# Gated linear attention and ternary FFN on one core: o is transposed and measured before it is centred and gated, and two transposes move up in TensorE's order

## The reference, cut to what matters

```python
q, k, v = x @ Wq, x @ Wk, x @ Wv                      # 16 heads of 8
gate = exp(log_sigmoid(x @ Wgk1 @ Wgk2 + bgk2) / 16)
state = state * gate[..., None] + v[..., None] * k[..., None, :]   # over the 512 tokens
o = einsum('bhvk,bhk->bhv', state, q)
o = (o - mean(o)) / sqrt(var(o) + 1e-5) * gamma + beta             # over the 128 channels
r = (o * silu(x @ Wg)) @ Wout
x2 = layernorm(x + r)
f1 = silu(x2 @ w1 * s1) * (x2 @ w2 * s2)              # 512 wide
f2 = gelu(f1 @ h1 * s3); f3 = gelu(f2 @ h2 * s4)
out = layernorm(x2 + f3 @ w3 * s5)
```

## Time and profile before

| | |
|---|---|
| median of 3 runs | 179.19 us (178.98 to 179.69) |
| profiled execution | 179.29 us, of which 177.5 are the span of the profile |
| TensorE (PE) busy | 160.9 us, 91% of the span |
| VectorE (DVE) busy | 141.6 us, 80% |
| ScalarE (ACT) busy | 110.2 us, 62% |
| GpSimd (POOL) busy | 109.4 us, 62% |
| granted TensorE clock | full speed in all of the span |

### The profile page before, as it was taken

The page is one execution under the profiler, slowest core; times in us unless marked ns, Lnnn a source line. Parts: engine busy times, 40 slices in busy tenths (PEclk is TensorE's granted clock), DMA queues, the critical chain, the costliest instruction groups (busy, mean ns, idle before and its releaser), DMA issues.

```text
span 177.5 us, 2647 instructions
## 1 busy us (share of the span) xinstructions
PE 160.9 (91%) x778; PEld 119.3 (67%) x778; DVE 141.6 (80%) x306; ACT 110.2 (62%) x179; POOL 109.4 (62%) x97
## 2 busy tenths in 40 slices
PE   0899999999879999999899999989999999999980
PEld 0766657868657666877666778567666875887870
DVE  0689989968898997698999987999998895854062
ACT  4454889992147635478683508667935388995722
POOL 8705998969609689970577989609684420803132
PEclk9999999999999999999999999999999999999999
DMA  3999920244200000000000000000020000041112
GB/s 109 284 380 416 398 91 0 59 122 118 59 4 0 0 2 0 4 2 0 0 0 0 0 0 0 0 0 0 0 63 0 0 2 0 0 104 32 34 31 63
DMA packets 7455, 10.55 MB, mean 59 GB/s; under 512 B 753, under 2 KB 5394, under 8 KB 6930
## 3 DMA queue, kind: packets, MB, share of 16 engines
q1 hardware_dynamic: 6866, 7.50, 13.9%
q0 software_dynamic: 576, 2.88, 4.2%
HBM read 8.55 MB, written 1.84 MB: 58 GB/s over the span
## 4 chain that ended last, share of the span: by engine, by line
DVE 21%; PE 19%; issue 14%; ACT 6%; POOL 3%; DVEq 1%; POOLq 0%; ACTq 0%
DVE state L1097 6%; PE ffn L640 5%; PE ffn L631 4%; DVE f_lo L1196 3%; DVE y L1109 2%; PE att L564 2%; PE ffn L609 2%; ACT f_hi L917 2%; PE ffn L614 1%; ACT last_f L1053 1%; DVE x L1133 1%; POOL o_rstd L360 1%; PE att L537 1%; ACT f_hi L909 1%; DVE r_stats L1121 1%
## 5 line engine op out<-in xcount | busy, mean ns | idle before, releaser
L1097 DVE TENSOR_TENSOR_SCAN state<-gate,att 128x512 f32<-128x512 f32 x32 | 38.3, 1208 | 2.2 <-PE att L553 2.2
L382 POOL TENSOR_TENSOR f_lo<-full,f_hi 128x512 fp32r<-128x512 f32 x18 | 23.0, 1298 | 25.1 <-DVE full L1185 18.1
L917 ACT ACTIVATE f_hi<-ffn,vec_cols 128x512 fp32r<-128x512 f32 x24 | 16.5, 688 | 27.5 <-PE ffn L640 27.3
L631 PE MATMUL ffn<-f_hi,h_hi 128*128 128x512 f32 x96 | 28.1, 407 | 0.2
L640 PE MATMUL ffn<-f_lo,h_hi 128*128 128x512 f32 x96 | 26.1, 399 | 0.0
L341 POOL TENSOR_TENSOR u_tok<-kv_tok 128x1024 f32<-128x1024 f32 x12 | 25.6, 2141 | 0.1
L356 POOL TENSOR_TENSOR o_acc<-o_acc,y 128x512 f32<-128x512 f32 x16 | 20.7, 1293 | 7.6 <-DVE y L1109 7.5
L631 PEld LDWEIGHTS ffn<-f_hi,h_hi 128*128 128x128 f32 x96 | 17.6, 188 | 5.8 <-ACT f_hi L917 1.5
L553 PE MATMUL att<-ident,u_tok 128*128 128x128 f32 x128 | 19.3, 278 | 1.6 <-DVE state L1097 1.2
L640 PEld LDWEIGHTS ffn<-f_lo,h_hi 128*128 128x128 f32 x96 | 17.8, 188 | 3.7
L553 PEld LDWEIGHTS att<-ident,u_tok 128*128 128x128 f32 x128 | 15.4, 143 | 6.2 <-DVE state L1097 3.2
(11 more groups left out here) (182 smaller groups left out, 349.2 us busy)
## 6 DMA issues: line engine op xcount, KB each, us to landing
h_raw<-in_hT SPq DMA_DIRECT2D x2, 1024.0 KB, 12.3
h_hi<-in_hT POOLq DMA_DIRECT2D x2, 1024.0 KB, 12.2
x_tok<-in_x SPq DMA_DIRECT2D x4, 256.0 KB, 5.8
out<-out_tok SPq DMA_DIRECT2D x3, 256.0 KB, 2.3
w_raw<-in_w12T SPq DMA_DIRECT2D x1, 512.0 KB, 5.5
w_hi<-in_w12T POOLq DMA_DIRECT2D x1, 512.0 KB, 9.2
q_swap<-q_hi SPq DMA_DIRECT2D x3, 128.0 KB, 2.3
q_swap<-q_lo SPq DMA_DIRECT2D x3, 128.0 KB, 2.4
```

The costliest lines, as they stand in the source:

```text
L382: nc.gpsimd.tensor_tensor(lo[:, o], full_block(layer, o), hi[:, o].bitcast(F32), ALU.subtract).then_inc(pool_rested, 1)
L631: nc.tensor.matmul(bank[:], h_hi[:, layer - 1, c, tile(o)], src_hi[:, c], start=(c == 0), stop=False)
L917: nc.scalar.activation(hidden[layer][0][:, o], bank[:], ACT.Gelu, scale=scales[:, 1 + layer, o:o + 1]).then_inc(gelu_hi_ready, 1)
L1097: nc.vector.tensor_tensor_scan(state[:, k % 3], gate[:, b], A[2 + k % 2][:], 0.0, ALU.mult, ALU.add).then_inc(scanned, 1)
```

## The change

On TensorE, `transpose_o` stands ahead of `center_o`; `ffn_out_hi` is split in two, blocks 0 and 1 ahead of `transpose_x2` and blocks 2 and 3 behind it; and `transpose_u` of the next row's k = 0 moves from the start of `first_layer` to before `ffn_out_rest`. On VectorE, the statistics, mean and variance of o stand ahead of the gate. On GpSimd, `e_rstd_of` moves behind the outer products and r_rstd. VectorE gets one wait near the end, for the e_shift of the row before.

```diff
@@ GpSimd @@
             def attention_end(a, tiles, last_tiles):
                 o_rstd_of(a)
-                if a >= 2:
-                    e_rstd_of(a - 2)
                 outer_products(a + 1, tiles)
                 r_rstd_of(a)
                 outer_products(a + 1, last_tiles)
+                if a >= 2:
+                    e_rstd_of(a - 2)
...
@@ TensorE @@
-            def ffn_out_hi(b, with_lo):
-                bank_read(b, 2, 1)
-                for c in range(OB):
+            def ffn_out_hi(b, blocks, with_lo):
+                if 0 in blocks:
+                    bank_read(b, 2, 1)
+                for c in blocks:
                     pe.wait_ge(gelu_hi_ready, 2 * OB * b + OB + c + 1)
...
             def first_layer(b, f, with_lo, follows):
                 if follows:
-                    transpose_u(b + 1, 0)
                     transpose_u(b + 1, 1)
...
                 ffn_hidden(f, 2, 0, with_lo)
+                transpose_o(a)
                 center_o(a)
-                transpose_o(a)
                 ffn_hidden(f, 2, 1, with_lo)
...
-                ffn_out_hi(f, with_lo)
+                ffn_out_hi(f, (0, 1), with_lo)
                 transpose_x2(a)
+                ffn_out_hi(f, (2, 3), with_lo)
+                if follows:
+                    transpose_u(a + 1, 0)
                 ffn_out_rest(f)
                 first_layer(a, f, with_lo, follows)
 
             def rows(with_lo):
                 transpose_x2(0)
+                transpose_u(1, 0)
                 first_layer(0, None, with_lo, True)
...
@@ VectorE @@
                 last_sums(a)
                 rest(f, 1, 2)
+                o_token_stats(a)
+                o_mean_and_variance(a)
                 apply_gate(a)
-                o_token_stats(a)
                 rest(f, 1, 3)
-                o_mean_and_variance(a)
                 if e is not None:
                     e_mean_and_variance(e)
...
             e_statistics(B - 2)
+            dve.wait_ge(e_shift_ready, B - 2)
             e_mean_and_variance(B - 2)
```

## The result

| | before | after |
|---|---|---|
| median, us | 179.44 (178.98 to 179.85, 4 runs) | 182.03 (181.73 to 182.74, 4 runs) |
| ratio after/before | | 1.0157 [1.0114, 1.0199] |
| profiled execution, us | 179.29 (span 177.5) | 182.74 (span 180.9) |

The kernel became slower, by 1.57%. The forecast was 181.3, with a range up to 182.2. The median, 182.03, lies just under that top; 1.0157 times the 179.44 of the kernel before is 182.26, just over it.

A forecast was written before the change was run, and what follows sets the result against it. Bound taken: the turn from finished o to the next row's scans, a VectorE chain, with x_hi ending turn 3. Losses 1.07 + 0.7 + 0.3 = 2.07 us on 179.29 (181.36; 181.26 against the median) gave 181.3; range 178.4 to 182.2.

The forecast's parts named there:

- The hold: VectorE's two-SBUF-input variance additions wait until GpSimd's running outer product ends, delaying gate and project_out; block given 0.74.
- Turn 1: End of attention of x row 1: project_out 2.14 us later, scan 0 at 83.1 against 82.04, 1.07 lost.
- Turn 2: End of attention of x row 2: o_var and e_var held, scan 0 at 116.35 against 115.69, 0.7 us lost.
- Turn 3: End of attention of x row 3: nothing held, project_out 0.68 us later, x_hi starts 0.3 later.
- small pow: GpSimd's o_rstd beside e_var: unlike the long products, said not to hold a two-input addition (0.17 us).
- idle time of PE before project_out: Sign of being right: PE idle ahead of project_out, which starts some 2 us behind the first transpose's old place.
- late u: In the range's upper end: u late by up to 0.5 us in each of two turns.
- held e_var: VectorE in turn 2: e_var waits for the third outer product until 109.0, add_x 1.6 us later; takes another 0.33.
- u sooner: u's first block transposed ahead of ffn_out_rest: VectorE's wait before scan 0 falls, 0.6 us won in turns 1 and 2.
- late fourth product: GpSimd's fourth outer product, awaited by u's transposes, could queue up ffn_out_rest and yT: cost nothing, bounds 0 and 0.5.
- e_rstd's move: On GpSimd, behind the outer products: costs nothing by itself; 1.2 us only if GpSimd's idle time were gone.
- no block: Rival: variances not held, gate late only by the order; 0.75 us won, 178.5; chance 0.16.

The follow-up runs named there:

- e4: The changed kernel with VectorE's order of before (gate, statistics, rest of block 3, mean and variance); 178.86 us, 0.994 of the kernel before.
- e5: The changed kernel with the addition of eps moved from VectorE to GpSimd, ahead of its power; 178.41 us, 0.9933 of the kernel before.
- e6: The changed kernel with the second of GpSimd's outer products moved behind o_rstd in turns 1 and 2; 179.16 us, 0.9972 of the kernel before.
- e1: The changed kernel with the variance computed by a tensor_scalar with one SBUF input and two constants; 182.6 us, 1.015 of the kernel before.
- e7: The kernel before with only the ffn_out_hi split and transpose_u moved ahead of ffn_out_rest; 178.03 us, 0.992 of the kernel before.
- e11: The changed kernel with VectorE's mean and variance moved behind the gate and rest; 176.92 us, 0.9866 of the kernel before.
- e10: The changed kernel run once more, unedited, for the spread of its executions; 182.04 us, 1.0143 of the kernel before.
- e2: The changed kernel with e_rstd back behind o_rstd, ahead of the third outer product on GpSimd; 182.3 us, 1.0144 of the kernel before.
- e9: The kernel before with only o's new order: transposes ahead of centring, statistics, mean and variance ahead of the gate; 183.06 us, 1.0221 of the kernel before.
- e3: The changed kernel with six unused 128x512 matmuls on TensorE ahead of project_out in turns 1 and 2; 181.16 us, 1.0083 of the kernel before.

## Why the prediction was right in kind and short in size

**The hold: right.** o_var of turns 1 and 2 was to last over 1 us and end with POOL's second product; it lasted 1.50 and 1.28 and ended 0.02 and 0.03 behind it. Project_out was to start at 73.6 in turn 1; it started at 73.55. e_var was to be held until the third product ends, and was. Turn 3 was to be free of it, and was. e4, e5 and e6 took the hold of o_var away in three different ways, and each time the loss went with it; that it is the cause is shown. Its reason as I put it, two inputs in SBUF, was too narrow (e1). That the small pow holds nothing, read from one e_var, stands: in turns 2 and 3 of the kernel before, e4, e7 and e11 e_var runs beside o_rstd each time, in 0.16 to 0.17 us.

**Turn 1: 1.07 lost by the forecast; 0.94 without the fall of the clock, 2.50 with it.** This is the step that failed: for the end of the last gelu I carried 78.88 + 0.66 + 2.14 = 81.68 over from rows at full clock, so that layer 2 was late by project_out's delay and by nothing more. In e10, at full clock, that gelu ends at 81.77; in the profile of the result, with the fall, at 83.30. I had named the idle time of PE before project_out as a sign to look for, but gave it no price beyond itself. After 1.92 and 1.89 us of it the clock fell in two profiled executions (after, e2) and not in three others with 1.91 to 1.92 us (e1, e9, e10). That is a term of 0 to 1.56 us, in a step where my range had only the 0.5 for a late u. The sum without it is 1.7 (e10, e1), less than my 2.07. With it in half of the executions, an estimate from the mean clocks of e10, it is 1.7 + 0.8 = 2.5, near the 2.5 to 2.8 of the medians and ratios; e3, with TensorE kept busy, gives 1.45. What decides in which execution the clock falls stays open: e9 had 1.91 us of idle time too, and its median, 3.5 over, fits its stretches without a fall (+3.57).

**Turn 2: 0.7 forecast, 0.35 measured.** From the first transpose to e_var's end I had 6.67 and it took 6.65. Then add_x was to follow at 6.82, with e_minus in between, and started at 6.65, beside it; and scan 0 was to start 0.1 behind x_lo's end and started with it. Small overlaps of neighbours on VectorE, 0.3 us together. The price of the held e_var, 0.33 in the forecast, is 0.18 by e2, where r_var is held a little instead.

**Turn 3: 0.3 forecast, 0.46 measured.** Project_out came 3.13 behind the first transpose, for 3.02. The split of `ffn_out_hi`, which I costed at nothing, is worth 0.41 here: without it e9 loses 0.86. My step from the last gelu straight to x_hi held only because of the split. In e7, where layer 2 is not late, it is worth nothing (third stretch 31.11 for 31.09).

**u sooner: 0.6 for each turn, measured 0.71 and 0.72** (e7), and 0.78 and 0.66 as the difference of e9 and e10, of which the split has a part (x_lo 0.31 and 0.24 sooner). The late fourth product that I gave 0 to 0.5 cost nothing that can be seen.

**e_rstd's move: nothing by itself**, as forecast, save that it lets the third product run into e_var; with the gate first it pays, by a short r_var (e11).

**The rival "no block"**: 0.75 won by my sum; e5, the nearest kernel to it, wins 1.26 in the median and 1.55 in the stretches. Its time, 178.41, lies near the 178.5 only because the kernel before took 179.67 beside it. Some 0.2 of what it wins beyond the sum is u, and its gate has no addition ahead of it: project_out comes 2.74 behind the first transpose, not 3.02.

## What to carry to other kernels

When a small VectorE instruction on SBUF tiles moves, look at which GpSimd instruction runs beside its new place: it can be held for all that is left of that one, the trace shows it as a long instruction and not as idle time, and everything behind it in the queue pays. Put what other engines wait for ahead of such an instruction, not behind it; here one line moved turned +1.4% into -1.3% (e10, e11). And where a change opens an idle time of some 2 us on TensorE, put a possible fall of its clock into the range, even if the trace of before shows none.

## What of the hardware was not expected

- **A tensor_scalar with one SBUF input and two constants is held like an addition of two SBUF tiles**: 1512 and 1660 ns for 170 (e1), while four aggregations from one SBUF input beside the same kind of product took 0.36 us together.
- **The same idle time gives a fallen clock in one execution and not in another.** In the two profiles that have it, the clock fell 0.75 and 0.8 us behind project_out's start and stood at 0.50 for some 3.4 us; eight 128x512 matmuls took 3.51 instead of 2.11 us (after). The Trainium skill, page "TensorE: Matmul & The Clock Gate", section "What's actually happening", says that a monitor sets the clock by how busy the engine has been, and that it runs freely, not from the kernel's start. That one kernel comes out both ways (after and e10) agrees with it.
- **A held VectorE instruction gets in between two GpSimd instructions that stand back to back** (e6: 1.55 us, the rest of the first product, not of both).
